# Two-term reciprocals, one value product and two scalings on another engine, in a software-pipelined chain of four attention blocks

## The chip, the cores and the metric

The kernel runs on one core of a Trainium2 chip. The metric is the device time of one execution in microseconds (us), as the median of several runs. Five engines work side by side, each through its own list of instructions in order, and meet only at semaphores: TensorE (PE, matmuls), VectorE (DVE), ScalarE (ACT), GpSimd (POOL) and SyncE (SP, which here issues the transfers).

## The reference

The input is 64 images of 256 channels by 14x14 pixels in float32. Four blocks follow each other, and each block's output is the next one's input:

- Block 0: a batch norm; a depthwise 3x3 convolution and a 256-to-768 pointwise product that give q, k, v; k and v are resized bilinearly to 7x7; attention with 4 heads of 196 queries on 49 keys with a relative bias; a second depthwise and pointwise convolution; the residual; then batch norm, ReLU, a 256x256 product and the residual.
- Block 1: a group norm in 8 groups, then linear attention: `softmax(k)` over channels, `softmax(q)` over the 196 tokens, `context = k^T v`, `out = q context`, a projection, plus the normalized input.
- Block 2: a group norm in 32 groups, 8-head attention of 196 tokens on 196 (32 channels a head), a projection, the residual.
- Block 3: a group norm in 32 groups, one-head attention of 196 on 196 over 256 channels, a projection, the residual.

## The kernel before, in words

The images go in 32 pairs. Channels lie on the 128 partitions in two chunks (`KC = 2`), a pair's pixels side by side on the free axis (`N2 = 392` columns; one image is `TOK = 196`, half an image `HALF = 98` tokens). All four blocks of a pair stay on the chip.

**The timetable.** The work of one pair is cut into uses, such as `kv0` (keys and values of the first 98 tokens in block 1) or `t3_1` (the transposes of the third block's probabilities, second image). The tables `PE_AT`, `ACT_AT`, `DVE_AT`, `POOL_AT` and `SP_AT` (lines 38 to 84) give each use a slot on each engine that takes part in it. `SLOTS = 128` slots make one step of the loop. In a step, every engine goes through the slots 0 to 127 and, at slot `u`, does the use whose number is `u` modulo 128, for the pair that began `number // 128` steps ago. So a step holds each use once, for up to six different pairs, and a table says nothing but the order in which an engine does its uses, and how many pairs back. The slots of two engines are not aligned in time: an engine goes on as soon as the semaphore of its next use allows. `run` (line 411) writes the first and the last steps out, with what has no pair left out, and loops over those between.

**PSUM.** Four banks `a`, `b`, `c`, `e` are shared by the uses that `BANK_USES` (line 86) lists, in the order of PE's slots; four banks `ps_s` belong to block 2's scores (`sc`), turned probabilities (`tn`) and outputs (`av`). A product waits until the use before it in its bank has been read.

**Arithmetic on PE.** Plain float32 products (`product`) take two records a matmul in the trace. `split_product` writes float32 operands as a high and a low fp32r term, three one-record matmuls for each chunk; there ACT rounds the high term (`high`) and DVE subtracts it (`low`).

**What the change touches.**

- `resize` (line 536, POOL) makes the 7x7 images in `yr`, and copies each so that an image fills 128 columns with twice 64. `v0` on PE multiplies these, once for each image, and ACT copies head halves into the block-diagonal `v0` (line 716).
- `keys0` to `keys3` (line 605, POOL) divide block 1's exponentials by their row sums, before `ctx0` and `ctx1`. `probs3_0` and `probs3_1` (line 626, POOL) do so for block 3, before `t3_0` and `t3_1`.
- Block 2's row sums: DVE takes reciprocals (`rden`), PE turns them (`rt`), DVE copies them to `rt2` (line 1064). For each image PE spreads them over the 32 channels of a head with the 0/1 matrix `heads` (`rep0`, `rep1`), and DVE multiplies the attention's outputs `a2` by them into `an2` (line 1074), which `proj0` and `proj1` read.
- A group norm runs: statistics on DVE (`stats`), sums over groups on PE (`gn`), a copy on DVE, some twenty small dependent operations and four scalings on POOL (`normalized`), `high` on ACT, `low` on DVE, and then the products of the next block.

In the trace all products of `product` and `split_product` have line 1167; the transposes have 1217 (`tn`), 1295 (`t0`), 1402 (`rt`) and 1459 (`t3`).

Of the kernel before, what the change touches and what calls it, by code (L numbers as in the profile page):

```python
# [9 lines left out]
ALU = mybir.AluOpType  # L10
# [28 lines left out]
    "x": -128, "res": 204, "hop": 486, "hop_out": 665, "store": 691,  # L39
# [41 lines left out]
    "resize0": 64, "resize1": 73, "probs0": 146, "probs1": 164, "gn1": 301, "keys0": 347, "keys1": 356, "keys2": 365,  # L81
    "keys3": 374, "gn2": 393, "gn3": 640, "rows3": 667, "probs3_0": 694, "probs3_1": 722,
# [3 lines left out]
    "a": ("s0_0", "s0_1", "t0_1", "pw0", "gn1", "ctx0", "out1", "hq1", "rt", "gn3", "s3_0", "t3_0", "o3_0",),  # L86
    "b": ("k0", "t0_0", "kv0", "q1_0", "out0", "hk0", "rep0", "proj1", "v3_0", "q3_0", "v3_3", "t3_1",
          "o3_1",),
    "c": ("q0_0", "mlp0", "kv1", "kv3", "ctx1", "hq0", "hv0", "hk1", "hv1", "rep1", "v3_1", "q3_1",),
    "e": ("q0_1", "v0", "o0_0", "o0_1", "pw1", "mlp1", "kv2", "q1_1", "gn2", "proj0", "v3_2", "s3_1",),  # L90
# [31 lines left out]
def build(nc, a):  # L122
    ctx = ExitStack()
    with ctx:
# [46 lines left out]
        ws = {name: sb(f"ws_{name}", [128, 2, KC, columns], F32R) for name, columns in SPLIT.items()}  # L171
        bn_scale, bn_shift = sb("bn_scale", [128, 4]), sb("bn_shift", [128, 4])
# [20 lines left out]
        yr = sb("yr", [128, KC, 2, 2, 64])  # L193
# [44 lines left out]
        rt2 = sb("rt2", [H2, 2 * TOK])  # L238
# [40 lines left out]
        PER_READ = {"k0": 2, "v0": 2, "o0_0": 2, "o0_1": 2, "q1_0": 2, "q1_1": 2, "ctx0": 2, "ctx1": 2,  # L279
# [64 lines left out]
        resize_steps = Count("resize_steps", KC * 9)  # L344
# [13 lines left out]
        rden_done = Count("rden_done", 1)  # L358
        l3_less_steps = Count("l3_less_steps", 2 * 3)
# [98 lines left out]
        EARLY_STEPS = PLAIN + FOLDED + 6  # L458
# [65 lines left out]
        def _(pool):  # L524
# [11 lines left out]
            def resize(p, c):  # L536

                link = linker(pool, resize_steps, p, 9 * c)
# [15 lines left out]
                first = yr[:, c, :, 0, 0:T7].rearrange("p i (a b) -> p i a b", a=R7)  # L554
# [3 lines left out]
                alone()  # L558
                link(g.tensor_copy(yr[:, c, :, 1, 0:T7], yr[:, c, :, 0, 0:T7]))
# [33 lines left out]
            def step(t):  # L593
                for u in range(SLOTS):
# [10 lines left out]
                    for j in range(4):  # L605

                        p = pair_of(t, u, POOL_AT[f"keys{j}"])
                        if p is not None:
                            pool.wait_ge(k_rsum.sem, k_rsum.at(p, j + 1))
                            alone()  # L610
                            g.tensor_scalar(kv[:, j, 0:CH], kv[:, j, 0:CH], rk[:, j:j + 1], None, ALU.mult).then_inc(k_scaled.sem, 1)  # L611
# [14 lines left out]
                    for i in range(2):  # L626

                        p = pair_of(t, u, POOL_AT[f"probs3_{i}"])
                        if p is not None:
                            pool.wait_ge(l3_rsum.sem, l3_rsum.at(p, i + 1))  # L630
                            for tc in range(2):
                                j = 2 * i + tc
                                alone()
                                g.tensor_scalar(e3[:, j], e3[:, j], r3[:, j:j + 1], None, ALU.mult).then_inc(p3_done.sem, 1)  # L634
# [25 lines left out]
        def _(act):  # L660
# [10 lines left out]
            def split_weights():  # L671
                act.wait_ge(weights_in, WEIGHTS)
                for n, (high, low, src) in enumerate(early_sources()):
                    if n == PLAIN:
                        act.wait_ge(fold_filled, FOLDS)
                    s.copy(high, src).then_inc(early_high, 1)
                act.wait_ge(early_steps, EARLY_STEPS)

            def step(t):
                for u in range(SLOTS):  # L680
# [137 lines left out]

                    for g in range(GROUPS):
# [21 lines left out]
                        if p is not None:  # L841
                            act.wait_ge(*full(p, use))
                            if has_before(p):
                                act.wait_ge(*read(p - 1, f"rep{i}"))
# [19 lines left out]
                    for i in range(2):  # L864
                        use = f"s3_{i}"
                        p = pair_of(t, u, ACT_AT[use])
                        if p is not None:
# [3 lines left out]
                            for tc in range(2):  # L871
                                j = 2 * i + tc
                                s.activation(e3[:, j], tile(use)[0:HALF, of_image(tc)], ACT.Exp, scale=SCALE3,
                                             bias=nm3[:, j:j + 1], accum_out=s3[:, j:j + 1]).then_inc(emptied(use), 1)
# [11 lines left out]
        def _(dve):  # L886
# [58 lines left out]
            def step(t):  # L945
                for u in range(SLOTS):
# [118 lines left out]
                    for i in range(2):  # L1065
                        use = f"rep{i}"
                        p = pair_of(t, u, DVE_AT[use])
                        if p is not None:
# [3 lines left out]
                            for source in ends(f"av{2 * i}", f"av{2 * i + 1}"):  # L1072
                                dve.wait_ge(*read(p, source))
# [474 lines left out]
```

## Time and profile before

| | |
|---|---|
| median of 3 runs | 2321.23 us (2320.8 to 2322.84) |
| the profiled execution: its time | 2331.84 us |
| its span (first to last instruction) | 2329.6 us |
| PE busy | 2158.8 us, 93% |
| DVE busy | 1851.9 us, 79% |
| POOL busy | 1493.3 us, 64% |
| ACT busy | 1443.0 us, 62% |

Busy time is the union of an engine's instructions. The ends of matmuls are modelled, so for PE the distance between two starts says more than a duration. A wait is put down to the engine whose semaphore came last.

### The profile page before, as it was taken

To read this page: it belongs to the slowest core of one execution; us is meant where nothing else is said; L and a number is where in the kernel's file an instruction comes from. 1 tells how busy PE (TensorE), PEld (TensorE's weight loads), DVE (VectorE), ACT (ScalarE), POOL (GpSimd) and SP (SyncE) were. 2 spreads that over 40 slices of the span, in tenths; PEclk is the share of its full clock that TensorE was granted. 3 is DMA by queue.
4 is the path that set the end of the run, shared out by engine and by line. 5 is a ranking of instruction groups with operands and counts; after the bars stand their busy time and mean duration, and the time that the engine had idled before them with its cause. 6 is when DMAs were issued, how large, how long until landed. Compare 5 with 4: busy or idle time off the path is not lost. (4 is left out here: it accounts for less than half of the span.)

```text
span 2329.6 us, 59692 instructions
## 1 busy us (share of the span) xinstructions
PE 2158.8 (93%) x15488; PEld 1724.9 (74%) x15488; DVE 1851.9 (79%) x4359; ACT 1443.0 (62%) x4819; POOL 1493.3 (64%) x3274
## 2 busy tenths in 40 slices
PE   5679999999999999999999999999999999999987
PEld 4456777777777777778777777777777777777775
DVE  6678788888888888888888888888888888887542
ACT  2246666666666666666666676666667666666663
POOL 3665667676666767666676766667676666775422
PEclk8699999999999999999999999999999999999997
DMA  3000011000000000000000001000000001000000
GB/s 117 14 22 22 15 36 36 34 21 14 34 34 34 34 34 21 14 34 34 34 34 27 28 14 34 34 34 34 21 34 14 34 34 34 28 29 29 15 29 21
DMA packets 29829, 70.24 MB, mean 30 GB/s; under 512 B 6260, under 2 KB 7104, under 8 KB 29760
## 3 DMA queue, kind: packets, MB, share of 16 engines
q1 hardware_dynamic: 26928, 67.68, 8.3%
q10 hardware_dynamic: 2832, 1.73, 0.3%
q8 instruction: 33, 0.54, 0.1%
q14 instruction: 36, 0.29, 0.0%
HBM read 30.86 MB, written 12.85 MB: 19 GB/s over the span
## 5 line engine op out<-in xcount | busy, mean ns | idle before, releaser
L831 ACT ACTIVATE e<-ps_s,nm 98x196 f32<-98x196 f32 x1024 | 421.5, 431 | 80.6 <-DVE nm L955 80.6
L1159 DVE SCALAR_TENSOR_TENSOR y<-opad,w_dw,y 128x406 f32<-128x406 f32 x512 | 303.9, 646 | 0.0
L1140 DVE SCALAR_TENSOR_TENSOR y<-xpad,w_dw,y 128x406 f32<-128x406 f32 x512 | 297.9, 644 | 0.0
L955 DVE TENSOR_REDUCE nm<-ps_s 98x4 f32<-98x784 f32 x256 | 244.7, 969 | 54.8 <-PE ps_s L1167 52.3
L590 POOL TENSOR_SCALAR xn<-x,gn_scale,gn_shift 128x196 f32<-128x196 f32 x384 | 264.5, 701 | 21.3 <-POOL gn_shift L585 21.3
L568 POOL TENSOR_TENSOR gn_t<-gn_group 128x4 f32<-128x4 f32 x96 | 29.6, 308 | 325.6 <-DVE gn_group L1005 249.6
L838 ACT COPY pt<-ps_s 98x392 f32<-98x392 f32 x512 | 223.4, 508 | 13.5 <-PE ps_s L1217 13.4
L1093 DVE TENSOR_TENSOR xs<-xn,xs 128x392 fp32r<-128x392 f32 x192 | 133.0, 695 | 108.9 <-ACT xs L788 106.8
L831 ACT ACTIVATION_READ_ACCUMULATOR e<-ps_s,nm 98x1 f32 x1024 | 217.1, 212 | 0.0
L1217 PE MATMUL ps_s<-w_eye,e 98*98 98x98 f32 x2048 | 202.6, 252 | 2.9 <-ACT e L831 2.7
L1217 PEld LDWEIGHTS ps_s<-w_eye,e 98*98 98x98 f32 x2048 | 187.2, 131 | 8.8 <-ACT e L831 4.8
L1167 PE MATMUL ps_c<-ws_v,xs 128*98 128x256 f32 (+1 forms) x960 | 139.1, 292 | 36.6 <-DVE xs L1093 36.6
L788 ACT CAST xs<-xn 128x392 fp32r<-128x392 f32 x192 | 100.1, 525 | 94.7 <-POOL xn L590 88.9
L1167 PEld LDWEIGHTS ps_c<-ws_v,xs 128*98 128x98 f32 x960 | 118.4, 165 | 46.2 <-DVE xs L1093 26.5
L581 POOL TENSOR_SCALAR gn_t<-gn_t 128x4 f32<-128x4 f32 x288 | 115.9, 403 | 56.2 <-POOL gn_t L579 56.2
L611 POOL TENSOR_SCALAR kv<-kv,rk 98x256 f32<-98x256 f32 x128 | 129.2, 1016 | 31.6 <-DVE rk L1023 31.1
L845 ACT COPY a<-ps_s 128x196 f32<-128x196 f32 x128 | 41.7, 326 | 163.7 <-PE ps_s L1167 163.7
L634 POOL TENSOR_SCALAR e<-e,r 98x196 f32<-98x196 f32 x128 | 105.7, 837 | 37.1 <-DVE r L1113 29.6
L755 ACT ACTIVATE kv<-kv,nmk 98x256 f32<-98x256 f32 x128 | 64.7, 507 | 100.4 <-DVE nmk L1017 100.3
L1167 PE MATMUL ps_s<-k,q 32*98 32x196 f32 x2048 | 118.8, 345 | 2.7 <-ACT k L807 1.4
L579 POOL TENSOR_TENSOR gn_t<-gn_t,gn_half 128x4 f32<-128x4 f32 x288 | 104.9, 364 | 22.6
L936 DVE BATCH_NORM_STATS2 gn_stats<-x 128x6 f32<-128x196 f32 x384 | 110.9, 351 | 9.2 <-DVE x L1049 5.3
(235 smaller groups left out, 5820.0 us busy)
## 6 DMA issues: line engine op xcount, KB each, us to landing
x_in<-in_x SPq DMA_DIRECT2D x32, 392.0 KB, 3.1
x_res<-in_x SPq DMA_DIRECT2D x32, 392.0 KB, 3.2
x2b<-x SPq DMA_DIRECT2D x32, 392.0 KB, 3.3
out<-x SPq DMA_DIRECT2D x32, 392.0 KB, 3.3
out_pairs<-out SPq DMA_DIRECT2D x32, 392.0 KB, 2.4
w_q<-in_q SPq DMA_DIRECT2D x3, 256.0 KB
w_k<-in_k SPq DMA_DIRECT2D x3, 256.0 KB
w_v<-in_v SPq DMA_DIRECT2D x3, 256.0 KB
```

The costliest lines, as they stand in the source:

```text
L581: link(g.tensor_scalar(t.t[:], t.t[:], 1.5, None, ALU.add))
L590: g.tensor_scalar(dst[:, c, of_image(i)], src[:, c, of_image(i)], t.scale[:, j:j + 1], t.shift[:, j:j + 1], ALU.mult, ALU.add).then_inc(t. ...
L611: g.tensor_scalar(kv[:, j, 0:CH], kv[:, j, 0:CH], rk[:, j:j + 1], None, ALU.mult).then_inc(k_scaled.sem, 1)
L831: s.activation(e2[:, j, tc], tile(use)[0:HALF, of_image(tc)], ACT.Exp, bias=nm2[:, j, tc:tc + 1], accum_out=den2[:, 2 * i + tc, h:h + 1]). ...
L838: s.copy(turned(j), tile(use)[0:HALF, 0:N2]).then_inc(emptied(use), 1)
L936: v.bn_stats(t.stats[:, j], src[:, j // 2, of_image(j % 2)]).then_inc(t.stat_steps.sem, 1)
L955: v.tensor_reduce(out=nm2[:, two], in_=ps_s[0:HALF, two, 0:N2].rearrange("p b (c n) -> p b c n", c=2), axis=AX.X, op=ALU.max, negate=True) ...
L1093: v.tensor_tensor(dst[:, 1, c], src[:, c], dst[:, 0, c], ALU.subtract).then_inc(gn[n].low.sem, 1)
L1140: v.scalar_tensor_tensor(out=dst, in0=window(xpad, c, k, CR), scalar=tap, in1=dst, op0=ALU.mult, op1=ALU.add).then_inc(conv1_steps.sem, 1)
L1159: v.scalar_tensor_tensor(out=dst, in0=window(opad, c, k, CR), scalar=tap, in1=dst, op0=ALU.mult, op1=ALU.add).then_inc(conv2_steps.sem, 1)
L1167: return nc.tensor.matmul(dst, lhsT, rhs, start=start, stop=stop)
L1217: last = nc.tensor.transpose(tile(use)[0:HALF, of_tile(sc, tc)], e2[:, j, tc, sc * HALF:(sc + 1) * HALF], eye[0:HALF, 0:HALF])
```

## The change

- The resized images are no longer copied; `yr` holds image 0 in columns 0 to 63 and image 1 in 64 to 127. One product of `v0` serves both images; ACT's copies take the image from the partition half, four of 64x128 in place of two of 64x256.
- Keys' scaling and block 3's probabilities' scaling go from POOL `tensor_scalar` to ACT `activation(Copy, scale=...)`.
- The turned reciprocals become two fp32r terms, `rt2[:, 0]` rounded by ACT and `rt2[:, 1]` the rest, by DVE. `heads` gets an fp32r copy, made once. `rep0` and `rep1` now stand for channel chunks: each is a product of 392 columns over the two terms, where each was two float32 matmuls of 196 columns.
- All slots of all engines and the lists of the banks are new; POOL has 8 uses in a step instead of 14.

```diff
-                link(g.tensor_copy(yr[:, c, :, 1, 0:T7], yr[:, c, :, 0, 0:T7]))            # POOL resize
...
-                        for hl in range(2):                                                # ACT v0
-                            half = slice(64 * hl, 64 * hl + 64)
-                            s.copy(v0[half, :, :, half], src[half, :, :, half]).then_inc(emptied("v0"), 1)
+                        for i in range(2):
+                            for hl in range(2):
+                                half = slice(64 * hl, 64 * hl + 64)
+                                s.copy(v0[half, i, :, half], src[64 * i:64 * i + 64, :, half]).then_inc(emptied("v0"), 1)
...
-                            g.tensor_scalar(kv[:, j, 0:CH], kv[:, j, 0:CH], rk[:, j:j + 1], None, ALU.mult)
+                            s.activation(kv[:, j, 0:CH], kv[:, j, 0:CH], ACT.Copy, scale=rk[:, j:j + 1])
...
-                                g.tensor_scalar(e3[:, j], e3[:, j], r3[:, j:j + 1], None, ALU.mult)
+                                s.activation(e3[:, j], e3[:, j], ACT.Copy, scale=r3[:, j:j + 1])
...
+                        s.copy(rt2[:, 0], tile("rt")[0:H2, 0:N2]).then_inc(rt_high.sem, 1)   # ACT rt
...
-                        v.tensor_copy(rt2[:], tile("rt")[0:H2, 0:N2])                        # DVE rt
+                        dve.wait_ge(rt_high.sem, rt_high.at(p, 1))
+                        v.tensor_tensor(rt2[:, 1], tile("rt")[0:H2, 0:N2], rt2[:, 0], ALU.subtract)
...
-                        for i in range(2):                                                   # PE v0
-                            last = product(tile("v0")[:, i * CH:(i + 1) * CH],
-                                           lambda k: yr[:, k, i].rearrange("p a n -> p (a n)"), lambda k: w["v0"][:, k])
+                        product(tile("v0")[:, 0:CH], lambda k: yr[:, k].rearrange("p i n -> p (i n)"),
+                                lambda k: w["v0"][:, k]).then_inc(filled("v0"), 1)
...
-                            for c in range(KC):                                              # PE rep
-                                last = mm(tile(use)[:, of_image(c)], w["heads"][:, c], rt2[:, of_image(i)], True, True)
+                            product(tile(use)[:, 0:N2], lambda k: heads[:, c], lambda k: rt2[:, k])
```

The new order of PE's uses in a step, from slot 0 (`use:steps back`):

```
hq0:3 gn1:1 av3:4 t0_1:1 t0_0:1 sc0:3 hv0:3 s3_0:5 hv1:3 hk1:3 s3_1:5 tn0_0,1,3,2:3 rep0:4 rep1:4 hq1:3 o0_1:1 proj1:4
o0_0:1 av0:3 proj0:4 sc1:3 kv0:2 t3_1:5 kv1:2 kv2:2 kv3:2 gn3:4 tn1_3,0,2,1:3 t3_0:5 q1_0:2 o3_0:5 q0_1:0 q1_1:2 sc2:3
ctx0:2 ctx1:2 q0_0:0 o3_1:5 out0:2 out1:2 av1:3 tn2_3,1,0:3 pw0:1 gn2:2 tn2_2:3 pw1:1 av2:3 k0:0 v3_0:4 sc3:3 s0_0:0
s0_1:0 v3_1:4 v3_2:4 q3_0:4 q3_1:4 mlp0:1 mlp1:1 tn3_3,2,1,0:3 v3_3:4 v0:0 rt:3 hk0:2
```

Of ACT's, the stretch that the prediction follows: `high1_0`, `o0_1`, `hq1`, `high1_1`, `o0_0`, `av0`, `probs3_0`, `probs3_1`, `t3_1`. POOL's whole list: `resize0`, `resize1`, `gn3`, `gn2`, `probs0`, `rows3`, `probs1`, `gn1`.

## Rows read from the trace of the kernel before

**Rows 1.** The page: busy time of PE; TensorE's granted clock in 40 slices.
```profile
PE 2158.8 (93%) x15488; PEld 1724.9 (74%) x15488; DVE 1851.9 (79%) x4359; ACT 1443.0 (62%) x4819; POOL 1493.3 (64%) x3274
...
PEclk8699999999999999999999999999999999999997
```

**Rows 2.** Windows: stretch, length, busy us (instructions) of each engine, granted clock, DMA.
```profile
60.00:260.00 200.00, 154.23 (x929) 115.25 (x931) 146.96 (x336) 92.34 (x293) 114.55 (x240) 0.87 0.07 21
...
1200.00:1268.06 68.06, 65.60 (x484) 52.59 (x483) 57.81 (x136) 44.78 (x150) 46.96 (x103) 1.00 0.08 28
...
2132.00:2200.00 68.00, 63.83 (x449) 50.32 (x446) 46.08 (x114) 42.75 (x150) 30.90 (x83) 0.97 0.08 25
2200.00:2329.60 129.60, 103.18 (x721) 86.84 (x719) 46.78 (x131) 61.88 (x215) 38.75 (x118) 0.85 0.07 29
```

**Rows 3.** Waits of PE, 420 to 2180 us: total us, times, longest.
```profile
PE ps_b L1459 <- POOL e L634: 33.3, 25, 1.4
PE ps_c L1167 <- DVE xs L1093: 21.9, 25, 2.2
PE ps_b L1167 <- DVE xs L1093: 8.2, 25, 0.5
```

**Rows 4.** Timeline of PE in one step: start, us, instructions, idle before.
```profile
1205.98 0.96 PE L1167 MATMUL ps_c<-ws_v,xs 128*98 128x258 f32 x6 [0.80 <-DVE xs L1093]
...
1224.91 1.33 PE L1167 MATMUL ps_c<-xs,ws_q 128*128 128x392 f32 x6
1226.09 1.23 PE L1167 MATMUL ps_b<-xs,ws_k 128*128 128x392 f32 x6
1227.16 1.89 PE L1167 MATMUL ps_e<-w_v,yr 128*128 128x256 f32 x8
1228.88 0.28 PE L1167 MATMUL ps_a<-gn_mine,w_group 128*128 128x8 f32 x2
...
1234.18 0.93 PE L1167 MATMUL ps_b<-rt,w_heads 8*128 8x196 f32 x4
1235.04 0.56 PE L1295 MATMUL ps_a<-w_eye,p 98*128 98x98 f32 x4
...
1243.12 0.93 PE L1167 MATMUL ps_c<-rt,w_heads 8*128 8x196 f32 x4
1244.36 1.60 PE L1167 MATMUL ps_b<-ws_kv,xs 128*98 128x512 f32 x6 [0.31 <-DVE xs L1093]
...
1274.04 0.96 PE L1167 MATMUL ps_c<-ws_v,xs 128*98 128x258 f32 x6 [0.80 <-DVE xs L1093]
```

**Rows 5.** POOL's two moved scalings, grouped over the same step: busy, mean ns.
```profile
L611 POOL TENSOR_SCALAR kv<-kv,rk 98x256 f32<-98x256 f32 x4 | 4.0, 998 | 0.5 <-DVE rk L1023 0.5
...
L634 POOL TENSOR_SCALAR e<-e,r 98x196 f32<-98x196 f32 x4 | 3.3, 845 | 0.3 <-POOL yr L559 0.3
```

**Rows 6.** ACT's instructions of these two shapes in the same step.
```profile
L831 ACT ACTIVATE e<-ps_s,nm 98x196 f32<-98x196 f32 x32 | 13.2, 430 | 2.2 <-DVE nm L955 2.2
...
L755 ACT ACTIVATE kv<-kv,nmk 98x256 f32<-98x256 f32 x4 | 2.0, 507 | 2.7 <-DVE nmk L1017 2.7
```

**Rows 7.** Timeline of DVE: the last sum of block 1 and its statistics.
```profile
1207.48 0.62 DVE L1049 SCALAR_TENSOR_TENSOR x<-ps_b,w_pb,xn 128x392 f32<-128x392 f32 x1
1208.31 1.15 DVE L936 BATCH_NORM_STATS2 gn_stats<-x 128x6 f32<-128x196 f32 x4 [0.21 <-DVE x L1049]
...
1210.02 0.16 DVE L943 TENSOR_TENSOR gn_mine<-gn_mine,gn_sq 128x4 f32<-128x4 f32 x1
```

**Rows 8.** Timeline of POOL: one group norm's start, and two groups of four scalings.
```profile
1202.80 1.97 POOL L590 TENSOR_SCALAR xn<-x,gn_scale,gn_shift 128x196 f32<-128x196 f32 x4 [0.22 <-POOL gn_shift L585]
...
1229.53 0.20 POOL L568 TENSOR_TENSOR gn_t<-gn_group 128x4 f32<-128x4 f32 x1 [2.21 <-DVE gn_group L1005]
...
1238.66 4.40 POOL L590 TENSOR_SCALAR xn<-x,gn_scale,gn_shift 128x196 f32<-128x196 f32 x4 [0.22 <-POOL gn_shift L585]
```

**Rows 9.** Timeline of DVE: the convolution steps beside the second of these.
```profile
1236.10 5.79 DVE L1140 SCALAR_TENSOR_TENSOR y<-xpad,w_dw,y 128x406 f32<-128x406 f32 x10
```

More of the change, by code:

```diff
@@ L38 @@
 SP_AT = {
-    "x": -128, "res": 204, "hop": 486, "hop_out": 665, "store": 691,
+    "x": -128, "res": 25, "hop": 358, "hop_out": 588, "store": 691,
 }
 PE_AT = {
[9 rows of a table removed]
[9 rows of a table added]
 }
 ACT_AT = {
[10 rows of a table removed]
[11 rows of a table added]
 }
 DVE_AT = {
[10 rows of a table removed]
[10 rows of a table added]
 }
 POOL_AT = {
-    "resize0": 64, "resize1": 73, "probs0": 146, "probs1": 164, "gn1": 301, "keys0": 347, "keys1": 356, "keys2": 365,
-    "keys3": 374, "gn2": 393, "gn3": 640, "rows3": 667, "probs3_0": 694, "probs3_1": 722,
+    "resize0": 0, "resize1": 16, "probs0": 64, "probs1": 96, "gn1": 240, "gn2": 304, "gn3": 544, "rows3": 592,
 }
 BANK_USES = {
[L86 to L90, printed above, removed]
[5 rows of a table added]
 }
@@ L276, in build @@
         gn = {1: GroupNorm(1), 2: GroupNorm(2), 3: GroupNorm(3)}
-        PER_READ = {"k0": 2, "v0": 2, "o0_0": 2, "o0_1": 2, "q1_0": 2, "q1_1": 2, "ctx0": 2, "ctx1": 2,
+        PER_READ = {"k0": 2, "v0": 4, "rt": 1, "o0_0": 2, "o0_1": 2, "q1_0": 2, "q1_1": 2, "ctx0": 2, "ctx1": 2,
                     "s3_0": 2, "s3_1": 2, "o3_0": 2, "o3_1": 2}
@@ L553, in resize @@
                     pool.wait_ge(*full(p - 1, latest("k0", "v0")))
-                first = yr[:, c, :, 0, 0:T7].rearrange("p i (a b) -> p i a b", a=R7)
+                first = yr[:, c, :, 0:T7].rearrange("p i (a b) -> p i a b", a=R7)
                 link(g.tensor_tensor(first[:, :, 0:6, :], x[:, :, 0:11:2, :], rs_e[:], ALU.add))
@@ L604, in step @@
                                             ALU.mult).then_inc(l0_probs.sem, 1)
[L605 to L611, printed above, removed]
                     p = pair_of(t, u, POOL_AT["rows3"])
@@ L676, in split_weights @@
                     s.copy(high, src).then_inc(early_high, 1)
+                s.copy(heads[:], w["heads"][:]).then_inc(early_steps, 1)
                 act.wait_ge(early_steps, EARLY_STEPS)
@@ L756, in step @@
                                          accum_out=sk[:, j:j + 1]).then_inc(k_exp_done.sem, 1)
+                        p = pair_of(t, u, ACT_AT[f"keys{j}"])
+                        if p is not None:
+                            act.wait_ge(k_rsum.sem, k_rsum.at(p, j + 1))
+                            s.activation(kv[:, j, 0:CH], kv[:, j, 0:CH], ACT.Copy, scale=rk[:, j:j + 1]).then_inc(k_scaled.sem, 1)
                     for c in range(KC):
@@ L817, in step @@
                             s.copy(v2[:, i].rearrange("p c n -> p (c n)"), tile(use)[0:HALF, :]).then_inc(emptied(use), 1)
+                    p = pair_of(t, u, ACT_AT["rt"])
+                    if p is not None:
+                        act.wait_ge(*full(p, "rt"))
+                        if has_before(p) and not comes_after("rt", latest("rep0", "rep1")):
+                            act.wait_ge(*full(p - 1, latest("rep0", "rep1")))
+                        s.copy(rt2[:, 0], tile("rt")[0:H2, 0:N2]).then_inc(rt_high.sem, 1)
                     for g in range(GROUPS):
@@ L843, in step @@
                             if has_before(p):
-                                act.wait_ge(*read(p - 1, f"rep{i}"))
+                                act.wait_ge(*read(p - 1, f"rep{g % 2}"))
                             s.copy(a2[:, i, g % 2], tile(use)[:, 0:TOK]).then_inc(emptied(use), 1)
@@ L874, in step @@
                                              bias=nm3[:, j:j + 1], accum_out=s3[:, j:j + 1]).then_inc(emptied(use), 1)
+                        p = pair_of(t, u, ACT_AT[f"probs3_{i}"])
+                        if p is not None:
+                            act.wait_ge(l3_rsum.sem, l3_rsum.at(p, i + 1))
+                            for j in (2 * i, 2 * i + 1):
+                                s.activation(e3[:, j], e3[:, j], ACT.Copy, scale=r3[:, j:j + 1]).then_inc(p3_done.sem, 1)
                         use = f"t3_{i}"
@@ L1060, in step @@
                     if p is not None:
-                        dve.wait_ge(*full(p, "rt"))
-                        if has_before(p) and not comes_after("rt", latest("rep0", "rep1")):
-                            dve.wait_ge(*full(p - 1, latest("rep0", "rep1")))
-                        v.tensor_copy(rt2[:], tile("rt")[0:H2, 0:N2]).then_inc(emptied("rt"), 1)
-                    for i in range(2):
-                        use = f"rep{i}"
+                        dve.wait_ge(rt_high.sem, rt_high.at(p, 1))
+                        v.tensor_tensor(rt2[:, 1], tile("rt")[0:H2, 0:N2], rt2[:, 0], ALU.subtract).then_inc(emptied("rt"), 1)
+                    for c in range(KC):
+                        use = f"rep{c}"
                         p = pair_of(t, u, DVE_AT[use])
@@ L1071, in step @@
                                 dve.wait_ge(*full(p - 1, latest("proj0", "proj1")))
-                            for source in ends(f"av{2 * i}", f"av{2 * i + 1}"):
+                            for source in ends(f"av{c}", f"av{2 + c}"):
                                 dve.wait_ge(*read(p, source))
-                            v.tensor_tensor(an2[:, i].rearrange("p c n -> p (c n)"), tile(use)[:, 0:N2],
-                                            a2[:, i].rearrange("p c n -> p (c n)"), ALU.mult).then_inc(emptied(use), 1)
+                            v.tensor_tensor(an2[:, :, c], tile(use)[:, 0:N2].rearrange("p (i n) -> p i n", i=2),
+                                            a2[:, :, c], ALU.mult).then_inc(emptied(use), 1)
                     for c in range(KC):
@@ L1270, in step @@
                         pe.wait_ge(*free(p, "v0"))
[L1271 to L1275 removed]
+                        pe.wait_ge(resize_steps.sem, resize_steps.at(p, 8 * KC))
+                        product(tile("v0")[:, 0:CH], lambda k: yr[:, k].rearrange("p i n -> p (i n)"),
+                                lambda k: w["v0"][:, k]).then_inc(filled("v0"), 1)
                     for i in range(2):
@@ L1404, in step @@
                         last.then_inc(filled("rt"), 1)
-                    for i in range(2):
-                        use = f"rep{i}"
+                    for c in range(KC):
+                        use = f"rep{c}"
                         p = pair_of(t, u, PE_AT[use])
@@ L1411, in step @@
                                 pe.wait_ge(*read(p, source))
-                            for c in range(KC):
-                                last = mm(tile(use)[:, of_image(c)], w["heads"][:, c], rt2[:, of_image(i)], True, True)
-                            last.then_inc(filled(use), 1)
+                            product(tile(use)[:, 0:N2], lambda k: heads[:, c], lambda k: rt2[:, k]).then_inc(filled(use), 1)
                     for c in range(KC):
```

29 lines of the change are left out of this document (10 added, 19 removed), and 64 rows, old and new, of tables (ACT_AT, BANK_USES, DVE_AT, PE_AT).

## The prediction

> **What bounds the kernel now.** First the page's first part and its slices [rows 1]: PE is busy 93% of the span, the next engine 79%, and TensorE's granted clock is at its higher level (2.4 GHz) nearly throughout. So PE is the candidate, and the clock is no term except at the ends. Second, one step of the loop. In PE's timeline the same use (`v3_1`) starts at 1205.98 and at 1274.04 [rows 4]: a step takes 68.06 us. In a window of that length PE is busy 65.60, DVE 57.81, POOL 46.96, ACT 44.78 [rows 2]. PE lacks 2.46 us. Third, the waits of PE [rows 3]: three, each once a step. `t3_1` waits for POOL's scaling (33.3 us over 25 steps, 1.33 each), the first product of block 3 waits for DVE's low term (0.80 [rows 4]; its total, 21.9, holds one longer wait) and `kv0` for the low term of block 1 (0.31 [rows 4]). 1.33 + 0.80 + 0.31 = 2.44, all of what PE lacks. So a step is PE's work plus three waits, of which the largest is for work that the change takes from POOL.
>
> How many steps are so? From 60 to 260 us PE is busy 77%, at 2132 to 2200 still 94%, after 2200 80% and at a lower mean clock [rows 2]. I count 260 to 2200: 1940 / 68.06 = 28.5 steps. The other 390 us are filling and draining, where PE's work is partly hidden behind chains.
>
> **The change, part by part.**
>
> *The value product.* Its eight records run from 1227.16 to 1228.88 [rows 4], 1.72 us. Half goes: 0.86 us a step. The operands keep shape and type, so this term is firm.
>
> *The spreading of the reciprocals.* Before: 1234.18 to 1235.04, 0.86, and 1243.12 to 1244.36 less 0.31 of idle, 0.93 [rows 4]; together 1.79. After: four fp32r matmuls of 392 columns. A use of six such records with 128 weights lasts 1224.91 to 1226.09, 1.18, or 1226.09 to 1227.16, 1.07 [rows 4], 0.18 to 0.20 a record. I take 0.20, so 0.79 for four: a gain of 1.0. With 8 rows instead of 128 nothing in these rows says that a matmul becomes dearer or cheaper, since the float32 one of 196 columns with 8 rows takes 0.22 a record. Bounds: at 0.18 the gain is 1.07. If a record of 392 columns were to cost what the float32 use costs by column, (1.79/784) for each of 1568 columns, it would be 3.58 in all, a loss of 1.8. The nearest row by type and columns is the fp32r one.
>
> PE's work becomes 65.60 - 0.86 - 1.00 = 63.74 us a step.
>
> *POOL's scalings.* POOL loses 4.0 + 3.3 us [rows 5] and two copies of `yr`: 46.96 to about 39. ACT gets them. The nearest rows are its Exp of 98x256, 0.507, and of 98x196, 0.430, though from PSUM [rows 6]: 4 x 0.51 + 4 x 0.43 = 3.8 us. The rounding of the reciprocals is one more instruction of 392 columns (the shape of `rt`, 8x392), and `v0` is four small copies in place of two. I allow 0.5 each. Bounds for ACT's addition: 3 us (if SBUF sources are quicker) to 8 us (at POOL's prices, 7.3, plus the rest). ACT at 44.78 + 4.8 = 49.6, at most 53, is covered by a step of 64: no cost by load. It costs only where an instruction behind it in ACT's list is due (below). DVE's `rt` stays one instruction of 392 columns; DVE stays at 57.8, 90% of the new step.
>
> *The first wait, `t3_1`.* The chain was `s3_1`, DVE's maximum, ACT's Exp, DVE's reciprocal, POOL behind both `resize`. To price a distance in the new order I give every use of PE the distance from its start to the next one's, less idle, over the 67 timeline rows of the step whose ends are in [rows 4] (they sum to the 65.60). Between `s3_1` and `t3_1` PE then had 19.65 us of work, and waited 1.35 more; now it has 10.1. That half looks dangerous, but the chain's own part is short: DVE 1.0, Exp twice 0.43 and accumulator reads, about 1.2, the reciprocal 0.2, scalings 1.7. What decides is what stands before the scalings in ACT's list: `high1_1`, which waits for POOL's group norm 1. From `gn1` to `t3_1` PE has 19.5 us. POOL's chain for a group norm ran from 1229.53 to 1243.06 [rows 8], 13.5 us, and that was with the conv steps beside it. 0.5 to POOL, 13.5, then `high1_1` 0.5, `o0_0` 0.7, `av0` 0.3, four scalings 1.7 and 0.2 back to PE: 17.4 against 19.5. I expect no wait.
>
> *The other two waits.* `gn3` to the first product of block 3 had 17.2 us of work between; the new order gives 23.7, more than 17.2 + 0.8. `gn1` to `kv0` had 14.95 and waited 0.31; now 17.7. Both go. POOL no longer has the keys' scalings ahead of group norm 3, which helps the first.
>
> *What is late next.* The short distances of the new order: `t3_0` to `o3_0` has one use between, 1.16 us, for one ACT copy of 0.5 and two hand-overs. `out1` to `gn2` has 3.15 between (6.7 before). Its chain is, from DVE's rows, 1207.48 to 1210.18, 2.70 us [rows 7], so 0.2 to 0.4 of room if DVE is free at once. `mlp1` to `gn1` has 5.55, for 5.1 us of DVE's list (`mlp1`, both `low2`, `rden`, `sum0_1`, `stats1`): nearly nothing to spare. So waits of some tenths are likely in two or three places. I take 0.8 us a step, with 0 and 2.5 as ends: 0 because each chain just fits, 2.5 because that is what today's order, also laid out so, leaves.
>
> *SP.* `res` now stands right after `x`, ahead of `store`, `hop_out` and `hop`, and waits for the residual sums of the pair before. A load or store takes about 3 us, and by the slots everything queued behind it is due over 10 us later. Nothing for it.
>
> Here the Trainium skill has a rule that weighs on the POOL chain. The row first: four scalings of a group norm took 1.97 us with DVE mostly idle, and 4.40 us beside ten conv steps in a row [rows 8, 9]. "SBUF — State Buffer", in the section on the engine and AXI ports, says that GpSimd and a DVE instruction with two SBUF inputs exclude each other for a whole instruction. The trace agrees in direction: 0.5 against 1.1 us for one scaling, about one conv step of 0.58 of waiting each. By that rule the moved scalings lose this toll as well, since they leave POOL. And conv steps that the new order puts beside a group norm would lengthen it by up to 2.4 us, which the 2.1 us of room before `t3_1` just about holds. It does not change the sum.
>
> **The sum.** A step: 63.74 + 0.8 = 64.54, 3.52 less than 68.06 (1.86 work, 1.66 waits). Over 28.5 steps: 100.3 us. In filling and draining 3.5 more pairs' worth of PE work shrinks by 1.86, of which I count half: 3. The lags of first and last uses hardly move (PE's first product to last, 645 slots before, 650 after), so I add nothing else, with 15 us of uncertainty either way. The profiled execution took 2331.84 us: 2331.84 - 103 = 2228.5. The median of the runs shown lies 10.6 below that execution, so the same for the changed kernel: 2218.
>
> **The rivals.**
>
> 1. *New waits take the place of the old.* Work falls, waits stay at about 2.5 us. For it: DVE at 90% with its list in order; several distances were halved; the order of today was laid out too and kept 2.46. Against: all three present waits get more room. Saving 28.5 x 1.86 + 3 = 56: 2265, and with 4 us of waits 2308.
> 2. *The spreading isn't cheaper.* If PE ran the two terms at float32's price for a column, the work would be 65.60 - 0.86 + 1.79 = 66.53; with 0.8 of waits 67.3, 0.7 less than today: 2300. Against: every fp32r row of 392 columns runs at a third of it.
> 3. *The other side: POOL's group norm 1 holds `t3_1` and the rest through ACT.* All of it stands in one line: `gn1`, POOL's last use, behind `rows3` and `probs1`; `high1_1`; `probs3`; `t3_1`; then `kv0`'s successors. It decides once the chain from PE's `gn1` to the last scaling passes 19.5 us. I count 17.4. It becomes slower than before when the chain passes 19.5 + 4.3 = 23.8 (4.3 is 68.06 - 63.74). `rows3` waits for `v3_3`, which ACT reads behind `high2_1`, itself behind POOL's group norm 2: should this detour hold POOL for 8 us (a group norm's chain shifted by half), the chain is 25.4, a step 63.74 + 5.9 = 69.6, and the time 2321 + 28.5 x 1.6 = 2366. For it: POOL's durations are the least steady in the trace. Against: PE has 16.6 us between `gn2` and the products behind it for a chain of 11 to 13.5, so group norm 2 is through before `v3_3` is due.
>
> **How the numbers follow.** The forecast (waits of 0 to 1.6 us): 0.62, with 2195 to 2245 around 2218. Rival 1 (2245 to 2310): 0.23. Rival 2: 0.04. Rival 3: 0.07, most of it above today's time. Left, 0.04: causes unnamed, on both sides. A difference under 0.2% (4.6 us) can't be told from none; it would take a saving that ends within 5 us of zero: 0.03. Faster 0.89, slower 0.08. Range: the low end is no waits (63.74, 2195) less some of the 15 us of the ends, at 2192; the high end goes into rival 1, up to 2.9 us of waits, 2275.
>
> **What would show it.** A step of 64 to 65.3 us between two starts of the same use; PE busy 63.7 in it at most; the four `rep` matmuls 0.2 us apart and `v0` with four records in 0.86; no wait of `t3` on POOL; ACT near 49.5 and POOL near 39 in a step. The prediction is wrong if PE waits over 1.6 us a step, above all at `gn2`, `gn1`, `o3_0` or `t3_1`; if the fp32r records of `rep` cost over 0.3; or if filling and draining, now some 390 us, grow by over 15.

## The result, and the profile after

The changed kernel takes 2169.53 us, the median of 4 runs (2168.79 to 2170.37), against 2321.88 (2320.80 to 2322.84, also 4). The ratio is 0.9344, with a 95% interval of 0.9328 to 0.936. The direction was forecast, but 2218 and the range of 2192 to 2275 were not enough of it: the gain is 152 us, not 104.

The profiled execution took 2170.37 us. The page's first part, the granted clock, and a window of one step, as in [rows 1, 2]:

```profile
PE 2076.3 (96%) x15232; PEld 1686.7 (78%) x15232; DVE 1820.4 (84%) x4359; ACT 1527.8 (70%) x5172; POOL 1278.3 (59%) x2954
...
PEclk8799999999999999999999999999999999999977
```

```profile
1007.74:1070.79 63.05, 62.98 (x475) 51.53 (x474) 56.56 (x137) 47.32 (x161) 40.56 (x92) 1.00 0.09 32
```

A step fell from 68.06 to 63.05 us, and PE is busy in nearly all of it. The clock is not the cause: the granted clock is 1.00, the higher level, in the step before [rows 2] and in this one. The waits of PE over 420 to 2050 us, which answer to [rows 3], are one line:

```profile
PE ps_s L1166 <- ACT a L841: 0.4, 1, 0.4
```

All three waits are gone, and no view shows one in their place. The edited products in PE's timeline, which answer to [rows 4] (start, us, instructions; a distance of two starts is the price):

```profile
1210.34 0.62 PE L1166 MATMUL ps_b<-rt,heads 8*128 8x392 f32 x2
1210.81 0.50 PE L1166 MATMUL ps_e<-rt,heads 8*128 8x392 f32 x2
1211.24 1.35 PE L1166 MATMUL ps_a<-xs,ws_q 128*128 128x392 f32 x6
...
1259.19 1.02 PE L1166 MATMUL ps_b<-w_v,yr 128*128 128x256 f32 x4
1260.05 0.50 PE L1399 MATMUL ps_e<-w_eye,rden 98*8 98x98 f32 x4
```

`v0` costs 0.86, as forecast. The spreading costs 0.47 + 0.43 = 0.90, 0.22 a record and not 0.20. The moved scalings, on ACT in the same step (busy, mean ns, idle before):

```profile
L746 ACT ACTIVATE kv<-kv,rk 98x256 f32<-98x256 f32 x4 | 1.9, 517 | 0.0
L875 ACT ACTIVATE e<-e,r 98x196 f32<-98x196 f32 x4 | 1.5, 450 | 0.0
```

Together 3.4 us of busy time, with means of 517 and 450 ns; the same work cost POOL 7.3 [rows 5]. The rows of ACT's Exp [rows 6] were the right price.

Where is the rest? The stores of the 32 pairs show the whole run step by step. For each kernel this is the view of the output tensor: all stores, then the registers' moves, which exist only in the 25 looped steps; their first and last starts. Before:

```profile
L517 SPq DMA_DIRECT2D out_pairs<-out x32: 337/364/379, 310.7 to 2326.8; - x32
L517 SPq MOVE out_pairs<-out x25: 29/29/29, 379.1 to 2014.2; - x25
```

After:

```profile
L519 SPq DMA_DIRECT2D out_pairs<-out x32: 337/356/1300, 304.9 to 2165.6; - x32
L519 SPq MOVE out_pairs<-out x25: 29/29/29, 368.1 to 1881.5; - x25
```

The 31 distances between stores shrank from 2016.1 to 1860.7 us in all, 5.01 each. The last six, in the draining, went from (2326.8 - 2014.2) / 6 = 52.1 to (2165.6 - 1881.5) / 6 = 47.35: 4.75 each, nearly a full step's gain. The first store came 5.8 us earlier.

### The profile page after: what moved, and what is told of

It is laid out like the page before. It is cut to its first block, busy times and chain, and to the rows that moved or that the text cites. A ratio compares the mean times of both kernels' runs of the same rounds, so it can differ in the third digit from the quotient of the medians.

```text
span 2168.3 us, 58678 instructions
## 1 busy us (share of the span) xinstructions
PE 2076.3 (96%) x15232; PEld 1686.7 (78%) x15232; DVE 1820.4 (84%) x4359; ACT 1527.8 (70%) x5172; POOL 1278.3 (59%) x2954
## 4 chain that ended last, share of the span: by engine, by line
PE 91%; DVE 3%; POOL 2%; issue 2%; ACT 1%; SPq 1%; DMA 0%; POOLq 0%; DVEq 0%; ACTq 0%
PE ps_c L1166 19%; PE ps_a L1166 17%; PE ps_e L1166 17%; PE ps_b L1166 17%; PE ps_s L1166 10%; PE ps_s L1216 8%; POOL gn_t L579 1%; PE ps_a L1292 1%; DVE y L1158 1%; PE ps_e L1454 0%; PE ps_e L1292 0%; PE ps_b L1454 0%; PE ps_e L1399 0%; SPq L475 0%; ACT e L827 0%
## 5 line engine op out<-in xcount | busy, mean ns | idle before, releaser
L590 POOL TENSOR_SCALAR xn<-x,gn_scale,gn_shift 128x196 f32<-128x196 f32 x384 | 353.2, 933 | 20.8 <-POOL gn_shift L585 20.8
L568 POOL TENSOR_TENSOR gn_t<-gn_group 128x4 f32<-128x4 f32 x96 | 34.3, 358 | 372.9 <-DVE gn_group L1006 286.5
L827 ACT ACTIVATION_READ_ACCUMULATOR e<-ps_s,nm 98x1 f32 x1024 | 231.6, 226 | 0.0
L1092 DVE TENSOR_TENSOR xs<-xn,xs 128x392 fp32r<-128x392 f32 x192 | 113.1, 589 | 41.7 <-ACT xs L778 39.3
L1166 PE MATMUL ps_a<-xs,ws_q 128*128 128x392 f32 x576 | 131.5, 363 | 0.4 <-ACT v L807 0.4
L778 ACT CAST xs<-xn 128x392 fp32r<-128x392 f32 x192 | 106.3, 554 | 31.4 <-POOL xn L590 31.3
L1166 PE MATMUL ps_s<-pt,v 98*32 98x196 f32 x2048 | 113.5, 339 | 3.5 <-ACT pt L834 2.7
L1166 PEld LDWEIGHTS ps_a<-xs,ws_q 128*128 128x128 f32 x576 | 102.0, 188 | 16.8 <-issue 7.7
L1166 PEld LDWEIGHTS ps_s<-k,q 32*98 32x98 f32 x2048 | 78.3, 163 | 46.8 <-issue 36.8
L579 POOL TENSOR_TENSOR gn_t<-gn_t,gn_half 128x4 f32<-128x4 f32 x288 | 95.7, 332 | 22.6
L578 POOL TENSOR_TENSOR gn_t<-gn_y 128x4 f32<-128x4 f32 x288 | 87.5, 304 | 23.1
```

Source lines behind the costliest of these rows:

```text
L579: link(g.tensor_tensor(t.t[:], t.t[:], t.half[:], ALU.mult))
L590: g.tensor_scalar(dst[:, c, of_image(i)], src[:, c, of_image(i)], t.scale[:, j:j + 1], t.shift[:, j:j + 1], ALU.mult, ALU.add).then_inc(t. ...
L827: s.activation(e2[:, j, tc], tile(use)[0:HALF, of_image(tc)], ACT.Exp, bias=nm2[:, j, tc:tc + 1], accum_out=den2[:, 2 * i + tc, h:h + 1]). ...
L1092: v.tensor_tensor(dst[:, 1, c], src[:, c], dst[:, 0, c], ALU.subtract).then_inc(gn[n].low.sem, 1)
L1166: return nc.tensor.matmul(dst, lhsT, rhs, start=start, stop=stop)
```

## The experiments

All compare a step in the loop, the distance of two starts of the same use. Times of a single run are marked so. Arithmetic and order were first parted: the new arithmetic in the old order, and the old arithmetic in the new order.

**Old order, new arithmetic.** The three edits, with all tables and banks of the kernel before.

```diff
 ACT_AT = {
+    "rt": 551, "keys0": 354, "keys1": 357, "keys2": 359, "keys3": 362, "probs3_0": 701, "probs3_1": 722,
```

> The new arithmetic (two-term spreading, one value product, both scalings on ACT) in the old order of all engines and banks; the moved uses get slots of their own in ACT's list. Theory A (the change's unforeseen gain of 0.6 us of PE work a step is the order's): PE's work in a step is 65.60 - 0.86 - 0.89 = 63.85 us, the wait of t3 on the scaling is gone, one or both waits on the low terms (0.80 and 0.31) stay: step 63.9 to 65.0, time 2190 to 2230. Theory B (the gain is the arithmetic's, and POOL's relief alone takes away the waits): PE's work 63.1, no waits, time 2170 to 2180.

Measured: 2265.83 us, ratio 0.9755 (0.9722 to 0.9788), a step of 65.93. Its window and PE's waits:

```profile
1058.53:1124.46 65.93, 64.49 (x475) 51.15 (x474) 57.44 (x136) 48.45 (x162) 39.57 (x93) 1.00 0.09 30
```

```profile
PE ps_b L1166 <- DVE xs L1092: 22.8, 23, 1.0
PE ps_a L1166 <- DVE gn_mine L944: 9.9, 24, 0.4
```

Without the new order, the three edits together end `t3_1`'s wait of 1.33 us and the listed 0.80 in front of block 3 (`v3_1`); that each wait fell to POOL's relief alone is not shown. The wait at `kv0` grows from 0.31 to 1.0, and one at `gn1` is new: 1.4 us of waits stay. PE's busy time falls by 1.11, not by the 1.75 that the two products' prices say (0.86 and 0.89). Neither theory gave 2266. Most steps of this kernel lie within 0.05 us of the one shown, but three of 22 took about 67.5.

**New order, old arithmetic.** The kernel before with the tables after, POOL's scalings in free slots.

```diff
 POOL_AT = {
+    "keys0": 276, "keys1": 277, "keys2": 278, "keys3": 279, "probs3_0": 625, "probs3_1": 626,
```

> The old arithmetic in the new order; POOL gets the keys' scalings between resize1 and gn3, and the probabilities' scalings after gn1. Theory A: PE's work 65.60 - 0.65 = 64.9 to 65.0 us a step, and the longer distances keep the waits under 1 us: step 64.9 to 66.0, time 2225 to 2260. Theory B: PE's work 65.6 and waits of 1 us or more, since POOL has its load again: step over 66.6, time 2277 or more.

Measured: 2228.67 us, ratio 0.9597 (0.9578 to 0.9616), a step of 64.69:

```profile
1036.62:1101.31 64.69, 64.54 (x483) 52.99 (x482) 57.30 (x137) 44.21 (x150) 46.75 (x103) 1.00 0.09 31
```

So the order alone removes the three waits, with POOL as loaded as before, and 1.06 us of PE's busy time too, though PE does the very same matmuls. Theory B is out. Theory A's step (64.9 to 66.0) was a little high. The new order is worth 3.4 us a step with the old arithmetic and 2.9 with the new; the arithmetic 2.1 in the old order and 1.64 in the new.

**The spreading in float32.** The changed kernel, `rep` as it was.

```diff
-                            product(tile(use)[:, 0:N2], lambda k: heads[:, c], lambda k: rt2[:, k]).then_inc(filled(use), 1)
+                            for i in range(2):
+                                last = mm(tile(use)[:, of_image(i)], w["heads"][:, c], rt2[:, 0, of_image(i)], True, True)
+                            last.then_inc(filled(use), 1)
```

> The changed kernel with the spreading of the reciprocals as four float32 matmuls of 196 columns again (the second term is still made, and is zero, but PE does not read it). Price of the spreading by the two traces: 1.79 against 0.90 us, so the step goes from 63.13 to 64.0 and the time from 2169.5 to 2197. If it costs over 1.5 us a step (2216 or more), the two-term spreading is also worth something to its neighbours on PE, against theory A; if under 0.5 (2185 or less), the trace's distances mislead.

Measured: 2190.16 us (one run), a step of 63.7, 0.65 to 0.70 more. The forecast had 1.00 for this edit. In this run's timeline the float32 spreading takes 1.52 us, with `rep0` and `rep1` side by side (1029.07 to 1030.59), where it took 1.79 in two places of the old order; the fp32r one takes 0.90. With the new arithmetic in the old order each fp32r `rep` takes 0.55 to 0.62. So the fp32r version saves about 0.6 in either order, and side by side both versions are some 0.2 to 0.3 cheaper.

**Scalings on POOL in the new order.** ACT's two blocks out, POOL's back in.

```diff
 POOL_AT = {
+    "keys0": 276, "keys1": 277, "keys2": 278, "keys3": 279, "probs3_0": 625, "probs3_1": 626,
...
-                            s.activation(kv[:, j, 0:CH], kv[:, j, 0:CH], ACT.Copy, scale=rk[:, j:j + 1])
+                            g.tensor_scalar(kv[:, j, 0:CH], kv[:, j, 0:CH], rk[:, j:j + 1], None, ALU.mult)
```

> The changed kernel with both scalings back on POOL: the keys' between resize1 and gn3, the probabilities' after gn1. Theory A (the new order alone has room for them): step at most 63.6 us, time 2170 to 2185. Theory B (the waits went because POOL was relieved): PE waits 1 us or more a step at t3_1, at ctx0 or at the products behind gn3, time over 2200.

Measured: 2181.87 us (one run), a step of 63.38. The waits of PE list 0.23 us a step as "issue", time behind which the profile shows no wait, and nothing else but 0.2 us once. Theory A holds: moving the scalings is worth 0.33 us a step once the order has room. In the old order `t3_1`'s wait of 1.33 us ended with the edits that hold this one.

**Why does the order change PE's own time?** In PE's timeline products of float32 and fp32r had other distances beside their own type, and the new order changes type 22 times a step instead of 34. That was theory C. The first test adds changes (PE's order in four places, slots exchanged accordingly):

```diff
-s0_0 s0_1 v3_1 | hv1 hk1 s3_1 | tn0_0 tn0_1 tn0_3 tn0_2 rep0 rep1 | rt hk0
+s0_0 v3_1 s0_1 | hv1 s3_1 hk1 | tn0_0 tn0_1 rep0 tn0_3 tn0_2 rep1 | hk0 rt
```

> The changed kernel with four uses of PE moved by one to three places, so that PE changes 30 times a step between float32 and fp32r matmuls, where it changes 22 times; nothing else differs. Theory C (each change between the two types costs PE about 0.09 us: with the old arithmetic 12 changes fewer went with 1.06 us less of PE's work): PE's work 63.0 + 0.7 = 63.7 us a step, time 2190 to 2195. Theory D (PE's work fell because in the new order the semaphores of its uses come earlier, so that weights are loaded ahead; the type doesn't matter): PE's work stays at 63.0 to 63.1, and only a wait in the trace can lengthen the step.

Measured: 2187.36 us (one run), a step of 63.57, no wait. 0.52 us more looks like theory C, but by place it is not. In the uses' distances the swaps `s0_1`/`v3_1` and `hk1`/`s3_1` sum to nothing (the second gives 0.14 on one and takes 0.14 on the other). The four turns `tn0` and the two `rep` alone went from 2.34 (1208.90 to 1211.24 in the changed kernel) to 2.83 (1218.18 to 1221.01 here):

```profile
1218.18 0.84 PE L1217 MATMUL ps_s<-w_eye,e 98*98 98x98 f32 x8
1219.10 0.62 PE L1167 MATMUL ps_b<-rt,heads 8*128 8x392 f32 x2
1219.65 0.88 PE L1217 MATMUL ps_s<-w_eye,e 98*98 98x98 f32 x8
1220.46 0.62 PE L1167 MATMUL ps_e<-rt,heads 8*128 8x392 f32 x2
```

A `rep` between turns costs 0.55 and more. What changes there is the array's shape: 8 rows against 98.

**Fewer changes of type.** Two uses of PE moved:

```diff
-hv0 s3_0 hv1 hk1 s3_1 | sc1 kv0 t3_1 kv1
+hv0 hv1 hk1 s3_0 s3_1 | sc1 t3_1 kv0 kv1
```

> The changed kernel with t3_1 ahead of kv0 and s3_0 behind hk1: 18 changes of type a step instead of 22. Theory C: PE's work 62.65 us a step, and 2158 us if no wait comes in (t3_1 stands 1.5 us earlier, s3_0 2.6 us later). Theory D: 63.0 to 63.1, time 2168 to 2172.

Measured: 2227.01 us, ratio 0.9567 (0.955 to 0.9585). PE's busy time rose to 63.30 in a step of 65.06, where theory C wanted 62.65. The two moves brought waits on DVE instead, 28.4 us in 23 steps for `an` and 10.3 in 22 for `x`:

```profile
PE ps_b L1167 <- DVE an L1074: 28.4, 23, 1.3
PE ps_b L1455 <- DVE x L1084: 10.3, 22, 0.7
```

So two moves of one or two places cost 2 us a step; the order is that finely balanced.

**Types alone.** PE alone, a stream of matmuls.

```diff
+            for _ in range(12):
+                high(6)
+            for _ in range(12):
+                plain(2)
+            for _ in range(12):
+                high(6)
+                plain(2)
```

> PE alone, without any semaphore between its matmuls; nothing of the reference is computed, the input's first pair is stored. Twelve groups of six fp32r matmuls of 392 columns in a row, twelve of two float32 ones in a row, then twelve of each in turn; the same with four transposes of 98x98 in place of the two; then 24 single matmuls of each type, and 24 of each in turn. Theory C: a pair of groups in turn takes 0.15 to 0.2 us more than the two taken from their own rows. Theory D: the same, within 0.03 us.

```profile
47.58 13.23 PE L164 MATMUL ps_r<-xr,wr 128*128 128x392 f32 x72
60.64 15.96 PE L171 MATMUL ps_f<-xf,wq 128*128 128x392 f32 x48
76.14 1.52 PE L164 MATMUL ps_r<-xr,wr 128*128 128x392 f32 x6
77.50 1.48 PE L171 MATMUL ps_f<-xf,wq 128*128 128x392 f32 x4
78.52 1.54 PE L164 MATMUL ps_r<-xr,wr 128*128 128x392 f32 x6
```

In rows of their own: 13.06 / 12 = 1.09 and 15.50 / 12 = 1.29, together 2.38. In turn: 78.52 - 76.14 = 2.38. A change of type costs nothing, and theory C is dead. The other distances in turn (1.36 for one, 1.02 for the other) sum to the same: only sums over neighbours may be read.

**Shapes alone.**

```diff
+            for name in "R P T S E K C RP TE RE SR SP ST KP KT CS ES".split():
+                if len(name) == 1:
+                    name += name
+                for _ in range(6):
+                    for one in name:
+                        uses[one]()
```

> PE alone again, no semaphores; nothing of the reference is computed, the input's first pair is stored. Seven kinds of use in the kernel's shapes, each twelve times in a row, then ten pairs of kinds in turn, six times each: R six fp32r 128x128 with 392 columns; P two float32 of the same; T four transposes of 98x98; S eight float32 with 32 rows, 98 columns of weights, 196 moving, in four row groups; E two fp32r with 8 rows and 392 columns; K six fp32r with 98 columns of weights, 512 moving; C four float32 with 98 rows, 256 moving. Theory E (a change of the number of rows, between 128 or 98 and 32 or 8, costs PE about 0.1 to 0.25 us, a change of type nothing): R-P, K-P, P-T and K-T in turn cost what they do in their own rows, within 0.03 us; R-E, T-E, S-R, S-P, S-T, C-S cost 0.2 to 0.5 us more a pair; E-S less than two such changes. Rival F (the changes cost nothing in PE, and the semaphores between uses make the difference): no pair over 0.05 us.

The start of T's, S's and E's own rows:

```profile
63.86 4.21 PE L179 MATMUL ps_f<-we,xf 98*98 98x98 f32 x48
68.00 8.22 PE L186 MATMUL ps_s<-xf 32*98 32x196 f32 x192
75.90 5.55 PE L193 MATMUL ps_r<-xr,wr 8*128 8x392 f32 x24
```

T's row, divided by 12, gives 0.345, and S's 0.658. E's can't be read so: the granted clock fell to its lower level inside it. Two windows (after the instructions of each engine comes the clock, 1.00 and 0.50), and the records of E that two short views hold, 16 in one and the last 3 of them in the other:

```profile
68.00:79.00 11.00, 11.00 (x210) 11.00 (x210) 0.00 (x0) 0.00 (x0) 1.00 0.01 1
79.20:81.30 2.10, 2.10 (x8) 1.73 (x6) 0.00 (x0) 0.00 (x0) 0.50 0.03 8
```

```profile
76.22 3.01 PE L193 MATMUL ps_r<-xr,wr 8*128 8x392 f32 x16
78.54 0.69 PE L193 MATMUL ps_r<-xr,wr 8*128 8x392 f32 x3
```

At the higher clock a record of E takes (78.54 - 76.22) / 13 = 0.178, so E takes 0.357. T and E, and S and R, in turn:

```profile
135.55 0.62 PE L193 MATMUL ps_r<-xr,wr 8*128 8x392 f32 x2
136.10 0.54 PE L179 MATMUL ps_f<-we,xf 98*98 98x98 f32 x4
136.57 0.62 PE L193 MATMUL ps_r<-xr,wr 8*128 8x392 f32 x2
```

```profile
162.93 0.92 PE L186 MATMUL ps_s<-xf 32*98 32x196 f32 x16
163.78 1.35 PE L165 MATMUL ps_r<-xr,wr 128*128 128x392 f32 x6
165.06 0.92 PE L186 MATMUL ps_s<-xf 32*98 32x196 f32 x16
```

T and E in turn take 136.57 - 135.55 = 1.02, 0.32 more than the two. S and R take 165.06 - 162.93 = 2.13, 0.38 more. S with P and S with C cost 0.4 more, S with T 0.32. E with S costs what the two do, within 0.02. K with P and K with T, and R with T in the run of types, stay within 0.05. Theory E holds: a change between products on 98 or 128 rows and products on 32 or 8 rows costs 0.16 to 0.2 us each way. (R with E ran at the lower clock and is left out. The uses `av`, with 32 columns of weights, were not among the kinds.)

The Trainium skill has a line that bears on this, in "TensorEngine Tiling (Array Packing)", Key Properties: "Changing tiling mode (not just tile) drains the TensorE". The trace agrees, if a product on 8 or 32 rows counts as another mode, and puts a price on it. The prediction had not weighed it.

**A whole step's list, on PE alone.** The old and the new order with each arithmetic, five steps of each, without semaphores, in the kernel's shapes but on a few stand-in operands, and with the other engines idle.

```diff
+            for names, new in ((BEFORE, False), (BEFORE, True), (AFTER, False), (AFTER, True)):
+                for _ in range(5):
+                    for name in names:
+                        use(name, new)
```

> PE alone with one step's whole list of uses, in the kernel's shapes and counts but without semaphores and on the same few operands; nothing of the reference is computed. Five steps each of: old order and old arithmetic, old order and new arithmetic, new order and old arithmetic, new order and new arithmetic. In the kernels PE's work in a step was 65.60, 64.50, 64.71 and 63.06 us. Theory E (the order's share lies in PE itself, in what stands next to what): the new order is 0.9 to 1.2 us shorter than the old with the old arithmetic and 1.2 to 1.6 with the new. Rival F (the share comes from the semaphores between uses, which come earlier in the new order): the orders differ by under 0.5 us, which is what the two to four changes of row group fewer account for at 0.11 to 0.2 us each.

One use (`rt`) marks the steps; the first and second line are one step apart, as are each later pair (the other steps of each list lie within 0.03 of these, but for the very first, 67.28):

```profile
139.30 0.50 PE L219 MATMUL ps_r<-we,xf 98*8 98x98 f32 x4
204.11 0.50 PE L219 MATMUL ps_f<-we,xf 98*8 98x98 f32 x4
...
397.04 0.50 PE L219 MATMUL ps_r<-we,xf 98*8 98x98 f32 x4
460.35 0.42 PE L219 MATMUL ps_f<-we,xf 98*8 98x98 f32 x3
...
714.63 0.50 PE L219 MATMUL ps_f<-we,xf 98*8 98x98 f32 x4
778.98 0.50 PE L219 MATMUL ps_r<-we,xf 98*8 98x98 f32 x4
...
1034.89 0.42 PE L219 MATMUL ps_r<-we,xf 98*8 98x98 f32 x3
1097.74 0.50 PE L219 MATMUL ps_f<-we,xf 98*8 98x98 f32 x4
```

| us a step | PE alone | PE busy in the kernel | beyond | waits | step |
|---|---|---|---|---|---|
| old order, old arithmetic | 64.81 | 65.60 | 0.79 | 2.46 | 68.06 |
| old order, new arithmetic | 63.31 | 64.49 | 1.18 | 1.44 | 65.93 |
| new order, old arithmetic | 64.35 | 64.54 | 0.19 | 0.15 | 64.69 |
| new order, new arithmetic | 62.85 | 62.98 | 0.13 | 0.07 | 63.05 |

In PE itself the order is worth 0.46 us a step, with either arithmetic: rival F's number, and about what two changes of shape fewer make (`rep0` and `rep1` now stand side by side) at 0.16 to 0.2 each (two changes more cost 0.49 in the run of more switches). Another 0.6 to 1.05 us of "busy" in the old order is there only where uses hand over through semaphores, and the new order is nearly free of it.

The two traces show where it sits. Laid beside each other use by use, the step of the kernel before and the same list on PE alone agree within 0.02 us in 49 of 57 stretches. The rest lies at the waits. The products ahead of `v3_1` (`out1` and `out0`), in the kernel and alone:

```profile
1270.38 1.53 PE L1167 MATMUL ps_a<-qe,cx 128*128 128x196 f32 x8
1271.74 1.49 PE L1167 MATMUL ps_b<-qe,cx 128*128 128x196 f32 x8
```

```profile
184.76 2.82 PE L170 MATMUL ps_r<-xf 128*128 128x196 f32 x16
187.28 1.02 PE L170 MATMUL ps_f<-xr 128*98 128x258 f32 x6
```

In the kernel `v3_1` starts at 1274.04 behind a listed wait of 0.80 [rows 4]: 1274.04 - 1270.38 - 0.80 = 2.86, against 187.28 - 184.76 = 2.52 alone. So 0.34 us more pass there than the listed wait says, and 0.06 more over the three uses from `v3_1` on. The same sum gives 0.20 at `t3_1` and 0.05 at `kv0`: 0.65 of the 0.79 lie at the three listed waits, and 0.08 at `k0`. In the kernel with the old order and the new arithmetic, 0.38 lie at the two listed waits, and 0.31 at `v3_1`, 0.23 at `hq1` and 0.10 at `k0`, where none is listed. So a wait costs more than its line in the view: the three cost 0.05 to 0.40 us more each, which the profile counts as busy time of PE. Whether the modelled end of the matmul before hides a part of the wait, or PE takes that long to start again, is not shown. Of the theories, E's share inside PE was too high (0.9 us or more); D, that the semaphores come in time in the new order, comes nearest for the rest.

## Why the prediction was wrong

**What held.** PE bounds the kernel before and after, and the clock is no term. `v0` gives 0.86. The three waits go. ACT bears the scalings, at 47.3 us a step (49.6 forecast), and POOL is at 40.6 (39). `res` ahead in SP's list costs nothing: no transfer appears among PE's waits. No rival came: there is no new wait in the loop, no fp32r record takes over 0.3 us, and no chain through group norm 1 shows.

**What failed.** The sum had 103 us of its own execution's time; that fell by 2331.84 - 2170.37 = 161.5. The 58 us are these:

| us a step | forecast | measured |
|---|---|---|
| arithmetic, in PE | 1.86 | 64.81 - 63.31 = 1.50 |
| order, in PE | 0 | 63.31 - 62.85 = 0.46 |
| busy beyond PE's work | 0 | 0.79 - 0.13 = 0.66 |
| waits | 2.46 - 0.8 = 1.66 | 2.46 - 0.07 = 2.39 |
| sum | 3.52 | 5.01 |

1. *"1.33 + 0.80 + 0.31 = 2.44, all of what PE lacks. So a step is PE's work plus three waits"*, and with it *"PE's work becomes 65.60 - 0.86 - 1.00 = 63.74"*: this reading took the profile's busy time as work, and work as a sum of prices that don't depend on the neighbours. On PE alone the old list takes 64.81. So the old order lost 68.06 - 64.81 = 3.25 us a step, almost all of it at its waits, and not 2.46; of the 0.79 that the busy time hid, 0.66 went. The order was put at nothing inside PE and is worth 0.46 there. The spreading is worth 0.64 (1.50 less `v0`'s 0.86), not 1.00: the fp32r record was priced rightly (0.178 alone, 0.18 to 0.20 forecast), but the old 1.79 held changes of shape and 0.07 of `kv0`'s wait, and the new version pays changes of shape too. Together -0.36 + 0.46 + 0.66 = 0.76 us, 22 us over 28.5 steps.
2. *"I take 0.8 us a step"* of new waits: there were none, 0.73 us a step and 21 us. The short distances (`t3_0` to `o3_0`, `out1` to `gn2`, `mlp1` to `gn1`) were all just enough. The prediction had found each chain to fit and then added waits on suspicion. In the run of fewer changes of type two small moves cost 1.7 us of listed waits, so the suspicion was not idle.
3. *"28.5 steps ... of which I count half"*: filling and draining gained 161.5 - 28.5 x 5.01 = 18.7 us, where the sum had 3. The 31 distances between stores each shrank by about a step's gain, also the last six (4.75). From the last looped store's move to the end (2014.2 and 1881.5 on) PE's busy time fell from 281.1 to 261.9 us and its idle time from 34.3 to 24.9, so in the draining too the gain is mostly busy time. A loop of 31 intervals, and not 28.5 steps and a discount, was the right multiplier: 15.7 us.
4. *"The median of the runs shown lies 10.6 below that execution, so the same for the changed kernel"*: the changed kernel's profiled execution lies only 0.8 above its median, so 10 us of the 161.5 were that one execution's own. This miss went the other way. What made it longer is not known.

22 + 21 + 16 - 10 = 49, the 48.5 us between 2218 and 2169.5.

## What to carry to other kernels

Where one engine is full, its busy time is not its work: run its list of instructions alone, without semaphores, and lay it beside the kernel's timeline use by use, before pricing an order by durations. The price of a wait is that difference, not the wait's line. Keep matmuls that use a few rows of the array beside each other. When a price is taken from a lone row, read the granted clock of that row first. When a software pipeline is bound by one engine in its loop, count a step's gain for every interval between outputs, the draining ones too. Waits that no chain asks for belong in the range rather than in the centre of a forecast; that they were nothing here, and 1.7 us after two small moves, shows how wide.

## What the runs showed of the hardware that was not expected

- An fp32r product of 392 columns takes 0.18 us and a float32 one of the same shape 0.65 (PE alone: 1.09 / 6, 1.29 / 2), and changing between them costs nothing (2.38 in turn, 2.38 apart). With 8 rows an fp32r one takes 0.18 too (2.32 / 13).
- Changing between products on 98 or 128 rows and products on 32 or 8 rows costs 0.16 to 0.2 us each way; 8-row and 32-row products in turn cost what they do apart, within 0.02.
- A wait of PE cost up to 0.40 us more than the profile lists for it (`v3_1`, above).
- POOL's scalings of 128x196 took 1.06 us on average in the new order, and 0.73 before. One of the twelve took 5.51 us, through a row of eight conv steps on DVE; the others took 0.50 to 1.22. No listed wait of PE answers to it.

```profile
L590 POOL TENSOR_SCALAR xn<-x,gn_scale,gn_shift 128x196 f32<-128x196 f32 x12 | 12.5, 1057 | 0.7 <-POOL gn_shift L585 0.7
```

The long one, from POOL's timeline, and the conv steps beside it, from DVE's:

```profile
1045.22 5.51 POOL L590 TENSOR_SCALAR xn<-x,gn_scale,gn_shift 128x196 f32<-128x196 f32 x1 [0.22 <-POOL gn_shift L585]
1045.85 4.50 DVE L1158 SCALAR_TENSOR_TENSOR y<-opad,w_dw,y 128x406 f32<-128x406 f32 x8
```
